# Filler products on TensorE around the start of a fused attention stage: one solid block taken out, two rows of single ones put in

## The reference

```python
x = x + tanh(g_xattn[0]) * _L0_xattn_ref(_layernorm(x), ctx, ctx, W_q, W_k, W_v, W_o)
x = x + tanh(g_ffn[0])   * _L0_ffn_ref(_layernorm(x), w_gate, w_up, w_down)
x = x + tanh(g_xattn[1]) * _L1_xattn_ref(_layernorm(x), ctx, ctx, gamma)
x = x + tanh(g_ffn[1])   * _L1_ffn_ref(_layernorm(x), W_router, ...)
```

```python
qk = jnp.einsum('bhdq,bhdl->bhql', qh, kh) * scale
sm = jax.nn.softmax(qk, axis=-1)
ret = jnp.einsum('bhql,bhdl->bhdq', sm, vh)
```

## Time and profile before

| | us |
|---|---|
| median of 3 timed executions | 675.91 |
| lowest, highest | 674.12, 676.22 |
| profiled execution: its own time | 673.21 |
| profiled execution: span | 671.5 |
| mean granted TensorE clock (1 is full) | 0.952 |
| TensorE busy | 603.9 (90%) |
| VectorE busy | 489.4 (73%) |
| ScalarE busy | 404.1 (60%) |
| GpSimd busy | 313.0 (47%) |

### The profile page before, as it was taken

How to read it: one execution, slowest core, us unless ns; L and a number is a source line. 1 busy time by engine, 2 the same in 40 slices (tenths; PEclk the granted TensorE clock), 3 DMA queues, 4 the chain that set the end, 5 groups by cost and what they waited for, 6 DMA issues and landing times. The chain is left out here.

```text
span 671.5 us, 16680 instructions
## 1 busy us (share of the span) xinstructions
PE 603.9 (90%) x4997; PEld 460.1 (69%) x4997; DVE 489.4 (73%) x999; ACT 404.1 (60%) x829; POOL 313.0 (47%) x430
## 2 busy tenths in 40 slices
PE   3688877999999966999999999999789699999995
PEld 2577765788888865655555555555478599999884
DVE  2877886788978796598899999996556634444756
ACT  3888884344434441488898888998645145555431
POOL 2455555023222557934675765753237334024254
PEclk9989997999999987699999999999969889999998
DMA  5434438400000014344444444440002435446344
GB/s 163 114 99 130 130 105 290 155 1 1 0 0 1 23 50 137 106 132 130 129 145 127 138 139 123 143 139 29 2 1 75 130 102 187 145 150 189 109 141 127
DMA packets 72601, 71.20 MB, mean 106 GB/s; under 512 B 12364, under 2 KB 68812, under 8 KB 72556
## 3 DMA queue, kind: packets, MB, share of 16 engines
q1 hardware_dynamic: 67324, 56.33, 28.2%
q0 software_dynamic: 5232, 14.29, 6.9%
HBM read 38.48 MB, written 31.36 MB: 104 GB/s over the span
## 5 line engine op out<-in xcount | busy, mean ns | idle before, releaser
L1420 DVE TENSOR_REDUCE a_smax<-a_s 128x2 f32<-128x512 f32 x256 | 164.7, 681 | 19.9 <-PE a_s L1348 15.1
L1242 ACT ACTIVATE a_prob<-a_st 128x512 f32<-128x512 f32 x256 | 141.8, 597 | 23.8 <-PE a_st L1343 22.7
L1348 PE MATMUL a_s<-kop,qop 64*128 64x256 f32 x512 | 106.3, 324 | 5.6 <-DVE a_smax L1420 3.4
L1343 PEld LDWEIGHTS a_st<-qop,kop 64*128 64x128 f32 x512 | 70.8, 187 | 56.8 <-issue 24.9
L1343 PE MATMUL a_st<-qop,kop 64*128 64x256 f32 x512 | 104.0, 315 | 0.6 <-DVE a_smax L1420 0.5
L1303 PE MATMUL a_pv<-a_prob,a_vt 128*32 128x256 f32 x1024 | 81.6, 391 | 3.2 <-ACT a_pv_sb L1227 1.7
L819 POOL TENSOR_TENSOR f_hs_lo<-f_kept,f_hs_hi 128x512 fp32r<-128x512 f32 x32 | 41.3, 1320 | 85.5 <-ACT f_hs_hi L769 85.5
L1348 PEld LDWEIGHTS a_s<-kop,qop 64*128 64x128 f32 x512 | 73.0, 193 | 7.9 <-DVE a_smax L1420 4.8
L1871 POOL DMA_INDIRECT sorted_rows<-m_xn,m_slot x32 | 33.5, 1047 | 46.1 <-PE m_gu L128 26.6
L126 PE MATMUL f_bank<-f_xt_hi,w_hi 128*128 128x512 f32 x128 | 51.2, 400 | 1.1 <-DVE w_raw L865 0.6
L127 PE MATMUL f_bank<-f_xt_lo,w_hi 128*128 128x512 f32 x128 | 50.5, 395 | 0.0
(11 more groups left out here) (263 smaller groups left out, 1663.4 us busy)
## 6 DMA issues: line engine op xcount, KB each, us to landing
qop<-qop_rows SPq DMA_DIRECT2D x64, 100.0 KB
kop<-kop_rows SPq DMA_DIRECT2D x64, 96.0 KB
sorted_rows<-x_all SPq DMA_DIRECT2D x2, 2944.0 KB, 15.4
qop<-sorted_rows SPq DMA_DIRECT2D x46, 128.0 KB, 2.3
expert_rows<-turned SPq DMA_DIRECT2D x46, 128.0 KB
kop_rows<-k_hi SPq DMA_DIRECT2D x32, 128.0 KB, 2.3
qop_rows<-q_hi POOLq DMA_DIRECT2D x30, 128.0 KB, 2.7
x_all<-in_x SPq DMA_DIRECT2D x4, 512.0 KB, 5.8
```

The source lines that it names most:

```text
L1242: act.activation(prob[:, u % 8], st_ps[BANK[u]][:], ACT.Exp, scale=SCALE1).then_inc(prob_ready, 1)
L1343: st = pe.matmul(st_ps[BANK[u]][:, c * D:(c + 1) * D], lhsT=kop[t.slot][rows, u // 2, c * P:(c + 1) * P], rhs=qop[t.slot][rows, u // 2], s ...
L1348: sm = pe.matmul(s_ps[BANK[u]][:, c * D:(c + 1) * D], lhsT=qop[v.slot][rows, w // 2, c * P:(c + 1) * P], rhs=kop[v.slot][rows, w // 2], st ...
L1420: dve.tensor_reduce(smax[:, v.slot, opposite(u)], s_ps[BANK[u]][:].rearrange("p (q n) -> p q n", q=2), AX_X, ALU.max).then_inc(smax_ready, 1)
```

## The change

Three things. Ten unread products of 128x512 are put behind the dense stage's last product, after a wait on a count (`silu_ready`) that was reached long before. The 18 in step 2 of the attention are taken out. One is put ahead of each of the 16 units of step 1.

```diff
@@ feed_forward0
+        AWAKE = 10
...
             down(Step(GROUPS - 1, 0, 1), 1)
+            pe.wait_ge(silu_ready, GROUPS * 8)
+            for i in range(AWAKE):
+                pe.matmul(g_ps[0][:], lhsT=w[0][:, 0, 0, i % 4, 0:P], rhs=xt[0][:, 0], start=True, stop=True)
@@ attention1
-        FILL = 18
...
                 for u in range(UNITS):
-                    if t.known and t.n == 0 and u == 4:
-                        keep_active(FILL)
+                    if v.known and v.n == 0:
+                        keep_active(1)
```

## The result

The changed kernel takes 680.12 us in the median (679.79 to 680.19, 4 runs) where before took 675.47 (674.12 to 676.22, 4 runs). The ratio is 1.007 with a 95% interval of 1.0053 to 1.0088: slower by 3.6 to 5.9 us, where 6.1 us less were forecast. The profiled execution has 680.11 us around a span of 678.3.

A forecast was written before the change was run, and what follows sets the result against it. The prediction took VectorE to set the pace in step 1 and TensorE to be the bound after the block of 18. Its terms, +0.3 - 0.3 - 6.1 = -6.1 us, took 675.91 to 669.8 us, range 667.0 to 674.0.

The forecast's parts named there:

- Part 1: Ten products behind the dense stage: next block starts 0.3 us later (0 to 0.6), and the clock need not fall at 259.2.
- first hole: TensorE's idle stretch behind the dense stage, 256.6 to 258.8, which the ten products were to fill.
- Part 3: Block of 18 in step 2 removed: 6.1 us won (6.1 to 6.4), its hidden operand loads costed at nothing.
- Part 2: One filler per unit in step 1: hidden at full clock, 0.86 us a unit at low clock; -0.3 us (-0.8 to +0.8).
- high clock, or a short fall: The forecast case for the clock from the ten products through step 1: 669.8 us, chance 0.60.
- rival (a): Clock falls in the second hole and one filler a unit doesn't lift it: 672.8 us, up to 674.9; chance 0.22.
- second hole: TensorE's wait for unit 0's maximum, after the scores of the first units: about 2.2 us expected with fillers.
- Rival (c): Clock low at entry of step 2 stays there without the solid block: slower, up to 681.6 us; chance 0.07.
- Rival (b): Tile 1's loads or negated maxima not ready at unit 8 of step 2: some 2 us lost, 671.9; chance 0.11.

The follow-up runs named there:

- part 3 alone: Kernel before with only the block of 18 products in step 2 taken out: 671.5 us, ratio 0.9925; repeated, 669.35 us, ratio 0.9921.
- short: Changed kernel with each single product of 128 columns in place of 512: 677.71 us, ratio 1.0022 to before.
- singles alone: Kernel before with only the 16 single products of step 1 added, block of 18 kept: 685.15 us, ratio 1.0143.
- later loads: Kernel with part 3 alone, its expert weights' loads issued behind the second half of the operand loads: 670.39 us, ratio 0.9931 to before.
- part 1 alone: Kernel before with only the ten products behind the dense stage added, block of 18 kept: 676.67 us, ratio 1.0015.
- parts 1 and 3: Changed kernel without its 16 single products in step 1: 671.31 us, ratio 0.9942 to before.
- half rows: Changed kernel with each single product of 64 rows at tile position 0 in place of 128 rows, same 512 columns: 673.61 us, ratio 0.9967 to before.
- pairs: Changed kernel with its 16 single products put as 8 pairs, before every second unit of step 1: 672.5 us, ratio 0.9967 to before.

## Why the prediction was wrong

**Part 1 was right.** The block start slipped by (259.71 - 257.16) - (258.81 - 256.63) = 0.37 us, forecast 0.3. The first hole was closed and the clock did not fall at 259.2.

**Part 3 was right.** The forecast was 6.1 us. With part 3 alone the marks lie 32.28 - 26.21 = 6.1 us closer (5.6 the second time), and the time falls by 5.1 us (3.2 to 7.0; 5.3 the second time). That step 2's own work brings the clock back holds: 276.9 with no filler. What doesn't hold in every execution is that a microsecond won there is one won at the end: the late transfer took it back in two of the profiled ones.

**Part 2 is the step that failed:** a filler and its two scores were put at "together 0.86" at the low clock, and at full clock at 0.45 and so "hidden". Measured: 1.45 and 0.86. The 0.43 and 0.23 were the distances of products among their own kind, and I added the columns of two kinds as if a change between them were free. It isn't: 0.29 us a change at the low clock, (1.45 - 0.86) / 2, as the short fillers show again. The Trainium skill (TensorE: Matmul & The Clock Gate, Part 2) says that the next product's weights load while the running one streams. That is so among the 18 of the block, from the second on, and the ten behind the dense stage, and not here, where a filler's load and that of the scores behind it begin only with their own product. The term was put at -0.3 us with an upper end of +0.8. It measured 9.4 less the 0.4 of part 1, and so +9.0.

**The forecast "high clock, or a short fall" failed too**, and rival (a), given 0.22, came true in its mechanism: the clock fell in the second hole, at 263.3, and stayed down for 23.9 us, with one filler a unit through step 1. The hole was only 0.65 us long, where 2.2 were worked out, since the changes had made the first units longer; so the fall isn't shown to come from the hole, and its cause stays open. Its price was wrong for the same reason as the term: it counted 0.86 a unit, and so came to a gain of 3.1. With 1.45 a unit, 12 x 0.59 = 7.1 us more, rival (a) would have given 675.9 - 3.1 + 7.1 = 679.9, and 680.1 was measured. That it is so close is in part luck, for two smaller errors of its sum cancel: the transposes took 0.6 us in place of 1.2, and the first four units of step 2 made up 0.1 in place of 1.1 (3.26 us where they had taken 3.37). So the case was seen, and the sum of it misjudged by one number above all. Even at full clock that number would have shown: 0.86 a unit is 0.25 over VectorE's 0.61, so the singles were not hidden in the best case either. By an estimate from these two numbers twelve units would have lost 3.0 us at full clock throughout, half of the gain.

Rival (c), slower by a clock that stays low deep into step 2, had the right sign for the wrong reason. The clock came back at 287.2, some 5 us into step 2, as it does without any filler. Rival (b), another bound at unit 8 of step 2, didn't come true: no profile has a wait for a transfer there. What it had in mind comes later: 0.9 us of waits for the negated maxima in the changed kernel, at 307.4, and 0.2 and 4.5 in the two profiled executions with part 3 alone. It costs part of the gain in some executions and isn't what decided.

The Trainium skill (same page, Part 1) has the clock's monitor run free of the kernel. From this rule the forecast took that the ten products would help in some executions and not in others. Counted from VectorE's addition, the fall came 2.4 to 3.5 us later in five profiled executions of kernels without the ten (before, part 3 alone twice, singles alone, later loads) and 5.9 to 6.9 us later in six with them (changed, part 1 alone, parts 1 and 3, half rows, pairs, short). So the place does move by about a microsecond, as the rule has it, but the ten products put it off by some 3.5 us on average, and the two groups don't overlap.

## What to carry to other kernels

In this kernel a filler was cheap only where it had the array shape of its neighbours, or stood in a row of its own: price it from rows in which its kind follows the other kind, never from a row of equals. Before paying for the clock, try without: where the work behind is dense, it lifts the clock itself, and leaving out the block of 18 that was to do it won 5 of its 6 us. Look behind the place too: here the freed time brought waits for a transfer in later steps. A clock that is held up through light work may fall at the next pause, in the middle of the heavy work.

## What the runs showed that I had not expected

- A change between a 128-row and a 64-row product costs 0.29 us at 1.2 GHz. At 2.4 GHz it is about 0.2, from 0.86 - 0.45 = 0.41 for two. In other words, a filler costs 0.73 us at the low clock where a row of its own kind says 0.43.
- Half-array fillers in the other tile position start within 0.01 us of the scores (265.06 and 265.07), and in the same position cost their columns alone, but in that kernel TensorE was busy for all of 9.70 us with the clock at 0.50:

```profile
263.80:273.50 9.70, 9.70 (x42) 7.07 (x42) 8.51 (x15) 3.47 (x6) 9.17 (x12) 0.50 0.65 189
```

- A busy share of 100% in the rows is thus no sign that the clock will come back. The changed kernel's 3.30 of 3.30 us at 0.50 says the same. It came back in step 1 only where full-array fillers stood in pairs.
